# A routed expert layer around attention on one core: the first expert computed for all tokens of two batches during the first threshold search, and the last projection and the turns of batch 2 placed later

## The chip, the core and the metric

The kernel runs on one core of a Trainium2 chip. The metric is the time of one execution on the device, in microseconds (us), lower is better. The engines are TensorE (PE), VectorE (DVE), ScalarE (ACT), GpSimd (POOL) and the queue of SyncE (SP), which only starts transfers. TensorE's clock has two levels, 1.2 and 2.4 GHz; the profile gives the granted clock as a share of the higher one.

## The reference

```
B, N, D = 4, 1024, 128        # E = 8 experts, I = 512, H = 16 heads of 8
def ffn(x):                   # k = N // E * 2 = 256 tokens for each expert of each batch
    affinity = softmax(x @ gate_w.T)              # over the experts
    gating, idx = top_k(affinity.transpose(0, 2, 1), 256)
    x_in = x[b, idx]
    h = silu(x_in @ w_gate[e].T) * (x_in @ w_up[e].T)
    return zeros_like(x).at[b, idx].add(gating * (h @ w_down[e].T))
x = x + 0.5 * ffn(layernorm(x))
x = x + attention(layernorm(x))                   # 3D rotary, softmax, projection
x = x + 0.5 * ffn(layernorm(x))
```

Everything is float32 at the inputs and outputs.

## The kernel before

The work is one program of hand-placed instructions for each engine, held together by semaphores. It has three stages: expert layer, attention, expert layer.

An expert layer works on halves of the batches: half 0 is batches 0 and 1 and half 1 is batches 2 and 3. A pass `it` (0 to 15 in the first layer, 16 to 31 in the second) is one expert on one half: 512 tokens (256 of each batch). Its tokens are gathered from DRAM by four indirect transfers on POOL (`gather`), turned on PE (`turn_tokens`), put through four gate and up matmul pairs with 512 columns (`gate_up(it, u)`), Silu on ACT, the product on DVE (`hidden`), and the down matmuls (`down`), which stand in the following pass. ACT or DVE scales the result (`outputs`), and POOL adds it to DRAM by four indirect transfers (`scatter`). Each engine has five slots in a pass, `between(it, 0)` to `between(it, 4)`, into which other work is put by the table `place`.

Before any expert of a half can run, its 256 largest affinities for each expert must be found. That is the front, `("f", hh, n)`: n = 0 to 3 turn the normalised tokens, n = 4 is the softmax of the logits, n = 5 to 7 turn the affinities, n = 8 to 17 are ten search rounds (DVE counts the affinities above a candidate in `compare`, PE adds the counts over partitions, DVE makes the next candidate), and n = 18 to 20 resolve ties and rank the chosen tokens. Then DVE writes one-hot rows for each expert (`onehots`), PE compacts the token numbers with them (`compact(j)`), and DVE reads off indices and gains (`pick(j)`), for which `gather(j)` waits. `("g", hh)` are the logits.

Half 0's front runs ahead of everything in the first layer, and half 1's is placed in the slots of passes 1 to 5. In the second layer half 0's front is placed in the last part of the attention, and half 1's in passes 17 to 22. `("p", b, g)` is the output projection of half g of batch b's attention, whose input DVE or POOL makes in `context`; those of batch 3 stand in pass 16. `moments`, `deviation` (a square root on ACT, which needs another function table than Silu), `scale_and_shift` and `normalise` are the layer norm.

ACT's tables switch between Sqrt, Exp and Silu. PE, DVE and ACT execute in order, so an instruction that waits holds up all behind it. `pY` is the one PSUM bank for down products.

Of the kernel before, what the change touches and what calls it, by code (L numbers as in the profile page):

```python
# [43 lines left out]
def tables():  # L44

    place = {}
    for n in range(NF):
        place[divmod(4 + n, 4)] = ("f", 1, n)
    place[1, 4] = ("g", 1)
# [4 lines left out]
    place[16, 2], place[16, 4] = ("p", 3, 0), ("p", 3, 1)  # L54
    for n, at in enumerate([(17, 3), (17, 4), (18, 0), (18, 1), (18, 3), (18, 4)] + [(19, k) for k in range(5)] +
                           [(it, k) for it in (20, 21) for k in range(4)] + [(22, 0), (22, 1)]):
        place[at] = ("f", 3, n)
    place[18, 2] = ("g", 3)
# [35 lines left out]
def program(nc, t, x1, out, zd, qk, vp, md, ud, dd, rd):  # L94
    ctx = ExitStack()
    with ctx:
# [127 lines left out]

        pairs = {u: (scr[:, u % 2, :], scr[:, 2 + u % 2, :]) for u in range(2, 6)}
# [12 lines left out]
        hid = [Pt[:, 2 + i, :, :].rearrange("p a (b n) -> p (a b) n", b=2) for i in range(2)]  # L238

# [64 lines left out]
        s_scat = [sem(f"scat{b}") for b in range(B)]  # L304

# [42 lines left out]

        def by_batch(a):
            return a.rearrange("(b c p) d -> b p c d", c=CH, p=P)  # L350
# [35 lines left out]
        def adds_before(j):  # L386
            return 256 * (j // RUN) + 32 * (j % E)
# [7 lines left out]
        def _(sp):  # L395
# [38 lines left out]
            for h in range(2):  # L434
                sp.dma_start(x1[h], t["x"][h * HB * N:(h + 1) * HB * N, :]).then_inc(s_copy, 16)
            for a, b in ((turn[:, :], t["turn"]), (wqT[:, :, :], t["wqkT"]), (wq[:, :, :], t["wqk"]), (bq[:, :], t["bqk"]),
                         (wv[:, :], t["wv"]), (wo[:, :], t["wo"]), (bvc[:, :], t["bv"]),
                         (bo[:, :], t["bo"].partition_broadcast(P)), (cos[:, :], t["cos"]), (sin[:, :], t["sin"])):
                sp.dma_start(a, b).then_inc(s_aconst, 16)
            store_z(2)  # L440
            store_z(3)

# [104 lines left out]
            for j in range(2, 11):  # L547
                load_weights(j)
            for b in range(2):
                sp.wait_ge(s_scat[b], 256)  # L550
                load_x(b, x1_in)
# [57 lines left out]
            write_out(2)  # L609
            write_out(3)  # L610
            load_weights(18)
# [6 lines left out]
        def _(pool):  # L618
# [11 lines left out]
            def gather(j):  # L630
                p = j % 2
                if j % E == 0:
                    pool.wait_ge(s_zst, 32 * (j // E + 1))
# [9 lines left out]
            def scatter(j):  # L643
# [3 lines left out]
                if j == 0:  # L647
                    pool.wait_ge(s_copy, 32)
                for k in range(HB * SH):
                    b = batches(j)[k // SH]  # L650
                    if k % SH == 0:
                        if j >= RUN and j % E == 0:
                            pool.wait_ge(s_out[b], 16)
                        if adds_before(j):
# [33 lines left out]
            def by_slot(hh):  # L688
# [3 lines left out]
                pool.wait_ge(s_upper, hh + 1)  # L692
                GP.tensor_tensor(to[:, :, :, 1, :], v, high, ALU.mult).then_inc(s_rest_above, 1)
# [136 lines left out]
            gather(0)  # L830
            gather(1)
            by_slot(0)
            pool.wait_ge(s_aconst, 16 * 10)
            GP.tensor_tensor(bvb[:, :], ones[:, :], bvc[:, 0:1].to_broadcast([P, D]), ALU.mult).then_inc(s_bvb, 1)
            for it in range(RUN):
                if it + 2 < RUN:
                    gather(it + 2)
                if it:
# [94 lines left out]
            for b in range(B):  # L933
                pool.wait_ge(s_scat[b], 512)

        @block.scalar
        def _(act):
# [22 lines left out]
            def front(hh, n):  # L960
# [7 lines left out]
                elif n < 7:  # L968
                    act.wait_ge(*written(key))
                    S.activation(affT[:, (n - 5) * 512:(n - 4) * 512], bank_of_use(key), ACT.Copy).then_inc(s_room, 1)  # L970
# [32 lines left out]
            def between(it, k):  # L1003
# [8 lines left out]
                if (it, k) == (0, 1):  # L1012
                    deviation(2)
                    deviation(3)
                if (it, k) == (0, 3):
                    normalise(2, 0, 4)
                if (it, k) == (0, 4):
                    normalise(2, 4)
                if (it, k) == (1, 0):
                    normalise(3, 0, 4)  # L1020
                if (it, k) == (1, 1):
# [16 lines left out]
                if (it, k) == (17, 1):  # L1038
                    deviation(11)
                if (it, k) == (17, 3):  # L1040
                    normalise(11, 0, 4)
                if (it, k) == (17, 4):
                    normalise(11, 4)

            def outputs(j):
                act.wait_ge(s_down, j + 1)
                if j % RUN >= 2:
# [12 lines left out]
            def expert(it):  # L1060
                last = it + 1 in (RUN, NIT)
                for u in range(IC):
# [7 lines left out]
                    if u == 1:  # L1070
                        between(it, 1)
                        if it - 1 in SEARCH:
# [14 lines left out]
            for n in range(2, 8):  # L1087
                front(0, n)
            act.wait_ge(s_lexp, 1)
            S.activation(warm[:, :], sd[:, 0:8], ACT.Silu)  # L1090
            turn_tokens(0)
            for it in range(RUN):
# [109 lines left out]
        def _(pe):  # L1202
# [14 lines left out]
            def front(hh, n):  # L1217
# [16 lines left out]
                elif n < 7:  # L1234
                    if n == 5:
                        pe.wait_ge(s_aff, hh + 1)
                    for k in range(4):
                        last = M.transpose(bank[:, k * P:(k + 1) * P], aff[:, 4 * (n - 5) + k, :, :].rearrange("p j r -> p (j r)"),
# [810 lines left out]
```

## Time and profile before

| | us |
|---|---|
| median of three timed runs | 1197.24 (1195.34 to 1200.41) |
| the profiled execution | 1198.01 |
| its span, first to last instruction | 1196.2 |
| PE busy | 1079.0 (90%) |
| DVE busy | 909.9 (76%) |
| ACT busy | 777.1 (65%) |
| POOL busy | 614.0 (51%) |

The span is what the rows are counted in. The profiled execution has 1.8 us around its span. A busy share is a mean over three stages with different limits, so each place has to be read by itself. The mean granted clock of TensorE is 0.95 of the higher level.

### The profile page before, as it was taken

The page shows a single profiled execution, that of the slowest core. Times are in us where ns is not written, and L with a number is a line of the kernel's source. Part 1 is how long each engine was busy: PE and PEld are TensorE (multiplying, and loading weights), DVE is VectorE, ACT ScalarE, POOL GpSimd, SP SyncE. Part 2 cuts the span into 40 slices and gives each one's busy share as a digit, 9 for nine tenths or more (in the row PEclk, how much of TensorE's full clock was granted, in tenths as well). Part 3 has the DMA queues.
Part 4 walks back from the last instruction along what each step waited for, and adds up shares of the span by engine and source line. Part 5 has one row for each costly group of instructions (what it writes and reads, how often), then busy time and mean ns, then how long its engine had stood idle before and what let it go on. Part 6 is the DMA issues. An engine that isn't in the chain of part 4 may idle for free.

```text
span 1196.2 us, 23692 instructions
## 1 busy us (share of the span) xinstructions
PE 1079.0 (90%) x8860; PEld 468.3 (39%) x8860; DVE 909.9 (76%) x1491; ACT 777.1 (65%) x1471; POOL 614.0 (51%) x626
## 2 busy tenths in 40 slices
PE   6189999898699999999999999999998889999993
PEld 6066666664232222222222222222222255666752
DVE  4746755465889999999999999999997454854441
ACT  3054322542668999999989999899999835222220
POOL 4047888777689401100005446555420187677886
PEclk7589999999799999999999999999999989999997
DMA  9015456458423411121211213102210125345553
GB/s 279 30 52 126 93 112 138 91 120 220 105 85 82 94 44 28 36 63 43 54 32 22 63 43 76 27 24 63 77 45 22 28 79 121 85 92 102 113 103 30
DMA packets 93066, 93.97 MB, mean 79 GB/s; under 512 B 14684, under 2 KB 70108, under 8 KB 92920
## 3 DMA queue, kind: packets, MB, share of 16 engines
q1 hardware_dynamic: 70424, 75.67, 22.5%
q0 software_dynamic: 22528, 16.79, 10.5%
q8 instruction: 70, 1.15, 0.4%
q14 instruction: 44, 0.36, 0.1%
HBM read 64.23 MB, written 30.13 MB: 79 GB/s over the span
## 4 chain that ended last, share of the span: by engine, by line
PE 43%; DVE 18%; issue 15%; ACT 13%; POOL 6%; SPq 2%; DMA 2%; another core or an unknown queue 0%; DVEq 0%; POOLq 0%; ACTq 0%
DVE mx L1919 12%; ACT Pt L1177 11%; PE pO L1506 7%; PE pA L1366 6%; PE pS L1354 6%; PE pS L1527 4%; PE pA L1442 3%; PE pO L1355 3%; PE pS L1355 3%; POOL out_dram L662 3%; DVE ge L1602 2%; PE pA L1334 2%; POOL xg L639 2%; PE pS L1270 2%; ACT U L1168 1%
## 5 line engine op out<-in xcount | busy, mean ns | idle before, releaser
L1919 DVE TENSOR_REDUCE mx<-pA 128x2 f32<-128x1024 f32 x512 | 585.3, 1214 | 16.4 <-PE pA L1442 15.5
L1177 ACT ACTIVATE Pt<-pS 128x512 f32<-128x512 f32 x1024 | 556.3, 596 | 31.6 <-PE pS L1527 23.2
L1506 PE MATMUL pO<-Pt,Vst 128*16 128x256 f32 x4096 | 322.2, 387 | 12.5 <-ACT U L1168 12.5
L639 POOL DMA_INDIRECT xg<-zd,idx x128 | 128.2, 1001 | 145.5 <-DVE idx L1726 74.3
L1067 ACT ACTIVATE Pt<-pS 128x512 f32<-128x512 f32 x128 | 76.3, 596 | 194.6 <-PE pS L1354 160.9
L1442 PE MATMUL pA<-Kst,Qst 48*128 48x512 bf16 x704 | 137.8, 389 | 17.6 <-DVE mx L1919 14.3
L1506 PEld LDWEIGHTS pO<-Pt,Vst 128*16 128x16 f32 x4096 | 68.1, 94 | 204.9 <-issue 108.3
L1527 PE MATMUL pS<-Qst,Kst 51*128 51x512 bf16 x704 | 138.2, 389 | 5.9 <-ACT Pt L1177 2.1
L729 POOL TENSOR_TENSOR mparts<-mx,onesm 128x32 bf16<-128x32 f32 x16 | 4.0, 252 | 268.3 <-DVE mx L1924 212.0
L1354 PE MATMUL pS<-Pt,wg 128*128 128x512 f32 x256 | 138.4, 623 | 2.7 <-issue 1.4
L1366 PEld LDWEIGHTS pA<-wd,Pt 128*128 128x128 f32 x960 | 113.1, 192 | 15.6 <-issue 15.5
L662 POOL DMA_INDIRECT x<-Pt,idx x64 | 101.8, 1591 | 23.9 <-issue 20.1
L1366 PE MATMUL pA<-wd,Pt 128*128 128x128 f32 x960 | 113.9, 276 | 0.0
L1753 DVE TENSOR_TENSOR Pt<-Pt,pS 128x512 f32<-128x512 f32 x64 | 44.0, 687 | 72.1 <-PE pS L1355 44.0
L1527 PEld LDWEIGHTS pS<-Qst,Kst 51*128 51x128 bf16 x704 | 34.3, 92 | 153.2 <-ACT Pt L1177 140.3
L1753 DVE TENSOR_TENSOR Pt<-Pt,pO 128x512 f32<-128x512 f32 x64 | 43.8, 684 | 34.6 <-PE pO L1355 20.9
L1355 PE MATMUL pS<-Pt,wu 128*128 128x512 f32 x128 | 68.6, 619 | 0.0
L1355 PE MATMUL pO<-Pt,wu 128*128 128x512 f32 x128 | 65.4, 592 | 0.0
L1527 PE MATMUL pS<-pair 51*128 51x512 bf16 x320 | 62.4, 386 | 1.1 <-ACT Pt L1177 0.4
L1442 PE MATMUL pA<-pair 48*128 48x512 bf16 x320 | 61.2, 378 | 0.6 <-DVE mx L1919 0.6
L1058 ACT ACTIVATE Pt<-pA 128x512 f32<-128x512 f32 x32 | 19.1, 597 | 64.5 <-issue 40.0
L1736 DVE TENSOR_SCALAR Pt<-pA,gain 128x128 f32<-128x128 f32 x72 | 20.3, 344 | 53.1 <-PE pA L1366 37.9
(234 smaller groups left out, 1236.6 us busy)
## 6 DMA issues: line engine op xcount, KB each, us to landing
wg<-w_gate_dram SPq DMA_DIRECT2D x32, 256.0 KB
wu<-w_up_dram SPq DMA_DIRECT2D x32, 256.0 KB
wd<-w_down_dram SPq DMA_DIRECT2D x32, 256.0 KB
qk<-parts SPq DMA_DIRECT2D x64, 96.0 KB
Kst<-qk SPq DMA_DIRECT2D x132, 32.0 KB
zd<-Z SPq DMA_DIRECT2D x8, 512.0 KB
vp<-pair SPq DMA_DIRECT2D x4, 1024.0 KB, 4.3
Vst<-vp SPq DMA_DIRECT2D x16, 256.0 KB
```

Source lines behind the costliest of these rows:

```text
L639: pool.indirect_dma_start(xg[p][:, k, :], None, zd[j // E % 2], bass.IndirectOffsetOnAxis(idx[j % 6][:, k:k + 1], 0)).then_inc(s_gath[p], 16)
L662: pool.indirect_dma_start(acc, bass.IndirectOffsetOnAxis(rows[j % 6][:, k:k + 1], 0), ye[j % 2][:, k, :], None, compute_op=ALU.add).then_i ...
L1067: S.activation(sg[:, u % 2, :], pG[u % 2], ACT.Silu).then_inc(s_silu, 1)
L1177: S.activation(Pt[:, s % 4, j, r * 512:(r + 1) * 512], pS[:, bank_of(k, 4 * s + 2 * j + r), :], ACT.Exp, scale=SCALE).then_inc(s_exp, 1)
L1354: M.matmul(pG[u % 2], wg[p][:, u * P:(u + 1) * P], xt[:, p, :], start=True, stop=True).then_inc(s_gate, 1)
L1355: M.matmul(pU[u % 2], wu[p][:, u * P:(u + 1) * P], xt[:, p, :], start=True, stop=True).then_inc(s_up, 1)
L1366: last = M.matmul(pY[:, k * D:(k + 1) * D], hid[p][:, i, k * P:(k + 1) * P], wd[p][:, i, :], start=(i == 0), stop=(i == IC - 1))
L1442: last = M.matmul(pA[ring[q, a] % 2][:, r, :], Qst[k][64 * r:64 * r + 48, j, c * P:(c + 1) * P], Kst[k][64 * r:64 * r + 48, j, half * 512: ...
L1506: last = M.matmul(pO[32 * h:32 * h + 16, cols], Vst[k][:, s % 8, h, :], Pt[:, s % 4, h // 2, (h % 2) * 512 + 256 * a:(h % 2) * 512 + 256 * ...
L1527: last = M.matmul(pS[:, bank_of(k, n + r), :], Kst[k][64 * r:64 * r + ROWS, j, (s % 8) * P:(s % 8 + 1) * P], Qst[k][64 * r:64 * r + ROWS, ...
L1753: V.tensor_tensor(hid[it % 2][:, u, :], sg[:, u % 2, :], pU[u % 2], ALU.mult).then_inc(s_hid, 1)
L1919: V.reduce_max(mx2[:, k, 2 * j:2 * j + 2, c, half], pA[ring[q, a] % 2][:, :, :], AX.X).then_inc(s_Ar, 1)
```

## The change

Two things are changed.

First, expert 0 of half 0 has no pass any more. All 2048 tokens of batches 0 and 1 go through it in 16 gate and up steps (`whole_step`) and four blocks of down products (`whole_down`), which are put between the search rounds of half 0's front. ACT does its Silu (`whole_silu`) and copies the down products out of PSUM unscaled (`whole_rows`). When the search is over, DVE makes a gain for every token that is zero where the token was not chosen (`whole_gains`), and in pass 1 adds gain times row to x (`whole_sum`); SP stores the sum as the first half of the layer's result, in place of the copy of x. The first pass is now `it` = 1. Batches 2 and 3 are normalised later, and half 1's front begins one slot on.

Second, in the second layer, batch 3's projections go from slots (16, 2) and (16, 4) to (16, 4) and (17, 1), with the DVE work that belongs to them; the one-hot rows of expert 18 go into slot (16, 0); the first instructions of half 1's front go from (17, 3) to (18, 0) and on, and end at (22, 1) as before.

```diff
     place = {}
-    for n in range(NF):
-        place[divmod(4 + n, 4)] = ("f", 1, n)
-    place[1, 4] = ("g", 1)
+    for n, at in enumerate([(1, 1), (1, 2), (1, 3), (1, 4), (2, 1), (2, 2), (2, 3), (2, 4)] +
+                           [divmod(4 + n, 4) for n in range(8, NF)]):
+        place[at] = ("f", 1, n)
+    place[2, 0] = ("g", 1)
...
-    place[16, 2], place[16, 4] = ("p", 3, 0), ("p", 3, 1)
...
+    place[16, 4], place[17, 1] = ("p", 3, 0), ("p", 3, 1)
...
 # SP
-            for h in range(2):
-                sp.dma_start(x1[h], t["x"][h * HB * N:(h + 1) * HB * N, :]).then_inc(s_copy, 16)
+            sp.dma_start(x1[1], t["x"][HB * N:2 * HB * N, :]).then_inc(s_copy, 16)
...
+            for b in range(HB):
+                sp.wait_ge(s_sum, b + 1)
+                for i in range(2):
+                    sp.dma_start(x1_in[b][:, 4 * i:4 * i + 4, :], X[:, b * CH + 4 * i:b * CH + 4 * i + 4, :]).then_inc(s_init[b], 16)
...
 # ACT
+            for n in range(13, 16):
+                whole_silu(n)
+            deviation(2)
+            deviation(3)
+            whole_rows(2)
+            normalise(2, 0, 4)
+            whole_rows(3)
+            act.nop().then_inc(s_xt, 1)
+            turn_tokens(1)
+            for it in range(1, RUN):
                 expert(it)
...
-                if (it, k) == (17, 1):
+                if (it, k) == (17, 3):
                     deviation(11)
...
 # PE
+            def whole_step(n):
+                t, i = divmod(n, IC)
...
+                if n >= 2:
+                    pe.wait_ge(*step_done(s_whole_hid, s_hid, n - 2))
+                M.matmul(pG[n % 2], wg[0][:, i * P:(i + 1) * P], ZT[:, t * 512:(t + 1) * 512], start=True, stop=True
+                         ).then_inc(*step_signal(s_whole_gate, s_gate, n))
+                M.matmul(pU[n % 2], wu[0][:, i * P:(i + 1) * P], ZT[:, t * 512:(t + 1) * 512], start=True, stop=True
+                         ).then_inc(*step_signal(s_whole_up, s_up, n))
...
+            for r in range(ROUNDS):
+                front(0, 8 + r)
+                whole_step(3 + r)
+                if r >= 2:
+                    whole_down(0, 2 * (r - 2), 2 * (r - 1))
+            front(0, 8 + ROUNDS)
+            whole_down(1, 0, 6)
+            front(0, 9 + ROUNDS)
+            whole_down(1, 6, 12)
+            front(0, 10 + ROUNDS)
+            whole_down(1, 12, 16)
+            whole_step(13)
...
 # DVE
+            def whole_sum(b):
...
+                for c in range(CH):
+                    last = V.scalar_tensor_tensor(X[:, b * CH + c, :], whole_y[:, b * CH + c, :], whole_gain[:, c, b:b + 1],
+                                                  X[:, b * CH + c, :], ALU.mult, ALU.add)
...
+            for r in range(ROUNDS):
+                front(0, 8 + r)
+                whole_product(3 + r)
+            for n in range(8 + ROUNDS, NF):
+                front(0, n)
+            all_onehots(1)
+            whole_product(13)
+            pick(1)
+            all_onehots(2)
+            whole_product(14)
+            pick(2)
+            whole_product(15)
+            all_onehots(3)
+            whole_gains()
             moments(2)
             moments(3)
```

On PE, in the first search, between two rounds (the matmul from `passed` is the round's sum over partitions) there was nothing. Before:

```order
L1243 MATMUL pA<-ident,affc 32x128 x4
L1247 MATMUL pA<-passed,same_try 128x1 x10
L1250 MATMUL pA<-cgt,same_row 128x1
L1251 MATMUL pA<-ceq,earlier 128x1
L1254 MATMUL pA<-csel,earlier 128x1
L1257 MATMUL pA<-identb,slotp 128x128
```

After, two rounds of the ten and the end of the search:

```order
L1312 MATMUL pA<-passed,same_try 128x1
L1501 MATMUL pS<-ZT,wg 128x512
L1503 MATMUL pS<-ZT,wu 128x512
L1516 MATMUL pA<-wd,Pt 128x128 x2
L1315 MATMUL pA<-cgt,same_row 128x1
L1316 MATMUL pA<-ceq,earlier 128x1
L1516 MATMUL pA<-wd,Pt 128x128 x6
L1319 MATMUL pA<-csel,earlier 128x1
L1516 MATMUL pA<-wd,Pt 128x128 x6
L1322 MATMUL pA<-identb,slotp 128x128
```

A step and two down products now stand behind each round's sum, and down products behind each of the last search matmuls.

On ACT, behind the last Silu of the whole expert, with what each row waits for:

```order
L1130 ACTIVATE Pt<-pS 128x512 [waits whole_hid,gate]
L987 ACT_TABLE_LOAD
L987 ACTIVATE sd<-mv,eps 128x8 [waits ve] x2
L1134 ACTIVATE scr<-pA 128x512 [waits whole_down]
L997 ACTIVATE Z<-X,shift,rstd 128x128 [waits zst,side,shift]
L997 ACTIVATE Z<-X,shift,rstd 128x128 x3
L1134 ACTIVATE scr<-pA 128x512 [waits down]
L1096 ACTIVATE Pt<-pA 128x512 [waits xtr]
```

The two copies of down products (blocks 2 and 3, L1134) stand behind the deviations of batches 2 and 3 (L987), which wait for DVE's statistics. All of this is new at this place.

On PE, in pass 16, from the compaction of expert 18 (L1334 before, L1399 after) on. Before:

```order
L1334 MATMUL pA<-columns,room 128x10 x16
L1306 MATMUL pA<-wo,scr 128x128 x4
L1354 MATMUL pS<-Pt,wg 128x512
L1355 MATMUL pS<-Pt,wu 128x512
L1344 MATMUL pA<-ident,xg 128x128 x4
L1354 MATMUL pS<-Pt,wg 128x512
L1355 MATMUL pO<-Pt,wu 128x512
L1306 MATMUL pA<-wo,scr 128x128 x4
```

After:

```order
L1399 MATMUL pA<-columns,room 128x10 x16
L1420 MATMUL pS<-Pt,wg 128x512
L1421 MATMUL pS<-Pt,wu 128x512
L1410 MATMUL pA<-ident,xg 128x128 x4
L1420 MATMUL pS<-Pt,wg 128x512
L1421 MATMUL pO<-Pt,wu 128x512
L1371 MATMUL pA<-wo,scr 128x128 x4
L1420 MATMUL pS<-Pt,wg 128x512
L1421 MATMUL pS<-Pt,wu 128x512
L1420 MATMUL pS<-Pt,wg 128x512
L1421 MATMUL pO<-Pt,wu 128x512
L1432 MATMUL pA<-wd,Pt 128x128 x8
```

The first projection (L1306, L1371) moved behind the turn of the next expert's tokens and the last gate pair; the second now stands behind these rows, in pass 17.

## Rows read from the trace of the kernel before

**Rows 1.** Head of the page, and its granted clock in tenths, in 40 slices.

```profile
span 1196.2 us, 23692 instructions
...
PEclk7589999999799999999999999999999989999997
```

**Rows 2.** Timeline of DVE, first search: start, duration, instruction, idle before.

```profile
26.55 1.28 DVE L1602 TENSOR_SCALAR_CACHE_REDUCE ge<-ZT,digits 128x1024 bf16<-128x1024 f32 x1 [2.43 <-ACT ZT L970]
...
29.05 0.16 DVE L1639 TENSOR_SCALAR step<-pA 128x1 int32<-128x1 f32 x1 [0.38 <-PE pA L1247]
...
31.41 0.16 DVE L1639 TENSOR_SCALAR step<-pA 128x1 int32<-128x1 f32 x1 [0.36 <-PE pA L1247]
...
54.86 0.29 DVE L1664 TENSOR_SCALAR upper<-pA 128x128 bf16<-128x128 f32 x1 [0.45 <-PE pA L1257]
...
66.55 0.64 DVE L1592 BATCH_NORM_AGGREGATE mv<-stats 128x2 f32<-128x6 f32 x8
```

**Rows 3.** Timeline of PE, first search and passes 0 to 3.

```profile
23.91 1.97 PE L1238 MATMUL pA<-ident,ZT 128*128 128x128 f32 x8 [3.18 <-DVE ZT L1682]
...
60.72 3.76 PE L1414 MATMUL pA<-ones 128*128 128x128 f32 x20
...
68.68 2.07 PE L1354 MATMUL pS<-Pt,wg 128*128 128x512 f32 x2 [0.69 <-issue]
...
79.58 1.02 PE L1354 MATMUL pS<-Pt,wg 128*128 128x512 f32 x2
...
81.73 1.02 PE L1354 MATMUL pS<-Pt,wg 128*128 128x512 f32 x2
...
83.45 1.95 PE L1366 MATMUL pA<-wd,Pt 128*128 128x128 f32 x16
85.23 0.60 PE L1223 MATMUL pA<-ident,Z 128*128 128x128 f32 x4
...
109.96 0.17 PE L1247 MATMUL pA<-passed,same_try 128*128 128x1 bf16 x1
```

**Rows 4.** Windows of one us: busy time of each engine, granted clock, DMA.

```profile
63.00:64.00 1.00, 1.00 (x9) 1.00 (x9) 1.00 (x6) 0.00 (x0) 0.91 (x1) 0.79 0.21 66
...
73.00:74.00 1.00, 1.00 (x3) 0.52 (x2) 0.26 (x1) 0.00 (x0) 0.00 (x0) 0.67 0.00 0
```

**Rows 5.** Timeline of ACT, pass 0: a table load and what follows it.

```profile
74.64 1.28 ACT L944 ACT_TABLE_LOAD   x1
75.93 0.49 ACT L944 ACTIVATE sd<-mv,eps 128x8 f32<-128x8 f32 x2
```

**Rows 6.** Timeline of PE, passes 16 to 22.

```profile
970.62 1.36 PE L1306 MATMUL pA<-wo,scr 128*128 128x128 f32 x8 [3.44 <-DVE scr L1805]
...
988.02 0.60 PE L1344 MATMUL pA<-ident,xg 128*128 128x128 f32 x4
...
1008.55 0.76 PE L1238 MATMUL pA<-ident,ZT 128*128 128x128 f32 x4 [2.31 <-DVE ZT L1682]
...
1019.65 0.16 PE L1247 MATMUL pA<-passed,same_try 128*128 128x1 bf16 x1
...
1025.57 0.16 PE L1247 MATMUL pA<-passed,same_try 128*128 128x1 bf16 x1 [1.26 <-DVE passed L1607]
...
1028.21 0.16 PE L1247 MATMUL pA<-passed,same_try 128*128 128x1 bf16 x1 [0.56 <-issue]
...
1057.42 0.22 PE L1257 MATMUL pA<-identb,slotp 128*128 128x128 bf16 x1
```

**Rows 7.** Timeline of POOL, passes 16 to 31.

```profile
981.85 0.95 POOL L639 DMA_INDIRECT xg<-zd,idx  x1 [0.30 <-issue]
...
1021.20 1.01 POOL L639 DMA_INDIRECT xg<-zd,idx  x1 [5.06 <-DVE idx L1726]
...
1064.80 1.01 POOL L639 DMA_INDIRECT xg<-zd,idx  x1 [2.45 <-issue]
...
1187.83 1.55 POOL L662 DMA_INDIRECT out_dram<-Pt,idxo  x1 [0.30 <-issue]
```

More of the change, by code:

```diff
@@ L304, in program @@
         s_scat = [sem(f"scat{b}") for b in range(B)]
+        s_whole_gate = sem("whole_gate")
+        s_whole_up = sem("whole_up")
+        s_whole_silu = sem("whole_silu")
+        s_whole_hid = sem("whole_hid")
+        s_whole_down = sem("whole_down")
+        s_whole_y = sem("whole_y")
+        s_whole_gain = sem("whole_gain")
+        s_sum = sem("sum")
+        s_init = [sem(f"init{b}") for b in range(HB)]
         s_bvb = sem("bvb")
@@ L347, in program, with step_done, step_signal, block_done @@
         s_out = [sem(f"out{b}") for b in range(B)]
+        def step_done(steps, passes, n):
+            return (steps, n + 1) if n < 15 else (passes, 4)
+        def step_signal(steps, passes, n):
+            return (steps, 1) if n < 15 else (passes, 4)
+        def block_done(blocks, passes, t):
+            return (blocks, t + 1) if t < 3 else (passes, 1)
+        def block_signal(blocks, passes, t):
+            return (blocks, 1) if t < 3 else (passes, 1)
         def by_batch(a):
@@ L1046, in outputs @@
                 act.wait_ge(s_down, j + 1)
-                if j % RUN >= 2:
+                if j % RUN >= 2 and j > 2:
                     for b in batches(j - 2):
@@ L1387, in expert @@
             def expert(it):
-                first, last = it in (0, RUN), it + 1 in (RUN, NIT)
+                first, last = it in (1, RUN), it + 1 in (RUN, NIT)
                 gate_up(it, 0)
@@ new lines, in whole_down @@
+            def whole_down(t, first, end):
+                if first == 0:
+                    pe.wait_ge(*step_done(s_whole_hid, s_hid, 4 * t + 3))
+                    if t == 0:
+                        pe.wait_ge(s_wd[0], 16)
+                        pe.wait_ge(*was_read(("f", 0, 4)))
+                    else:
+                        pe.wait_ge(*block_done(s_whole_y, s_ye, t - 1))
+                for m in range(first, end):
+                    k, i = divmod(m, IC)
+                    last = M.matmul(pY[:, k * D:(k + 1) * D], whole_hid[t][i][:, k * P:(k + 1) * P], wd[0][:, i, :],
+                                    start=(i == 0), stop=(i == IC - 1))
+                if end == 16:
+                    last.then_inc(*block_signal(s_whole_down, s_down, t))
@@ L1436, in _ @@
+            front(0, 9 + ROUNDS)
[3 more added lines that the diff above has]
+            whole_step(13)
+            pe.nop().then_inc(s_comp, 1)
+            compact(1)
+            whole_step(14)
+            compact(2)
+            whole_step(15)
+            whole_down(2, 0, 16)
+            whole_down(3, 0, 16)
+            pe.nop().then_inc(s_xtr, 1)
+            turn_tokens(1)
+            for it in range(1, RUN):
                 expert(it)
```

173 lines of the change are left out of this document (106 added, 67 removed).

## The prediction

> **What bounds the kernel now.** I read the page first for span and clock [rows 1], then the timelines of DVE and PE over the first 112 us [rows 2, 3], the one-microsecond windows for the granted clock [rows 4], ScalarE's table loads [rows 5], and PE and POOL over the second expert stage [rows 6, 7]. The attention stage between them is untouched and only shifts. The chain of waits names PE for the first stage and POOL's calls for the end.
>
> The first search, 26.55 to about 54.9, is a chain of DVE and PE: a round is 31.41 - 29.05 = 2.36 us, and PE does 0.16 us in it. TensorE is at 1.2 GHz nearly all through it and up to 73 us (the 5s in the head's clock line); each time it rises some 3 to 5 us after dense work resumes (dense work from 60.72, level up in the window 63 to 64; from 68.68, up in 73 to 74) [rows 3, 4]. From pass 0 on PE is nearly never idle: the first stage is bounded by PE.
>
> The second stage is different. POOL's calls run to the end of the span, back to back (0.3 us apart) from the gather at 1064.80, and PE is done long before the last call at 1187.83 [rows 7]. What sets the end is when expert 24's gather may start, which waits for the end of the second-half search (last PE result of it 1057.42). Before that, PE stalls 3.44 us for the context product at 970.62 and 2.31 us at 1008.55 [rows 6]; POOL idles 5.06 us before 1021.20 and 2.45 before 1064.80 [rows 7]. So work saved on PE in passes 16 to 22 is worth at most POOL's idle time there.
>
> **Part 1: the search that now carries expert 0.** One step is a gate and an up matmul of 512 columns: 1.72 us at 2.4 GHz (from 81.73 to 83.45), about twice that at 1.2 (the two matmul halves of a gate took 2.07 us at 68.68, those at 81.73 took 1.02). A block's down products are 16 of 128x128, 3.57 us: half of them stand between 83.45 and 85.23 [rows 3]. So 16 steps and 4 blocks are 27.5 + 14.3 = 42 us of PE at the high level; PE had 33 us from 20.7 to 54.
> Start: steps 0 and 1 begin at 20.73 (PE was free from there: the row at 23.91 less its 3.18 of idle), ahead of the transposes that stood at 23.91. At 1.2 GHz they take 6.9 us; if the level rises after 3.5 us, they end at 20.73 + 3.5 + (3.44 - 1.75) = 25.9. The transposes then run at twice the speed, and the first scan starts at 27.8, for 26.55: 1.25 us late (bounds 0.7 and 3.7: level up after 2.5 us, or not at all).
> Rounds: each gets a product on DVE behind the scan. The second-half search has such rounds: 1025.57 to 1028.21, 2.64 us [rows 6], so + 0.28 for nine rounds, 2.5, and 0.25 for the first. PE does 1.72 + 0.45 in a round, so it fits, if the clock is high.
> After the last round PE first finishes step 12 and two down products (1.72 + 0.45 = 2.2 us), while the tie count, which needs no scan, is ready before; the product there also waits for the end of block 0, and six down products (1.34) stand ahead of each of the next two search matmuls. By these pieces I estimate + 1.35 (bounds 0.3 and 2.5). Together the search ends 5.35 us later: the first scores of slots are read at 60.2, for 54.86 [rows 2].
> From there to the first sparse pass: DVE went from 54.86 to the end of the fourth statistics, 67.19, in 12.33 us. It gets three products, the last behind a PE step that stands behind the second compaction (together about 2.6) and the gains (0.3): 15.25. ScalarE has both deviations ahead of the copy of block 2, and the copy frees the only bank that block 3 can use. So PE waits from about 11.9 to 16.3 after the slot scores, 4.4 us, and that is long enough to lose the clock (after 2.31 us without work it was lost at 1008.55: the four transposes there took 0.76 us, those at 85.23 took 0.60). Block 3 then takes 4.8 us (3.6 at the high level, 7 at the low); copy, token turn and copy 2.2. The first gate of pass 1 comes 23.35 us after the slot scores, where it came 79.58 - 54.86 = 24.7.
> Pass 1 loses pass 0's down (3.57) but has three of the four half normalisations on ScalarE, which set its length: 10.65 us. Pass 2 gets the logits matmul (1.1), and the softmax has one slot less to hide in (0.9), as has the first scan (0.4): 17.65 to the first search matmul of the second half. 23.35 + 10.65 + 17.65 = 51.65, where rows 2 and 3 give 109.96 - 54.86 = 55.1. Gain 3.45, less 5.35: the first stage is **1.9 us slower** (range 6 slower to 2 faster). It removes a whole pass of 15 us and pays it back in the search, in PE's wait and in the dense work. The two sums on DVE (16 operations, some 5 us) lie in passes 1 and 2, where it waits for PE. The copy of x that is gone from the queue freed nothing that waited; the stores that take its place are needed only at the first scatter, 25 us on. Moving x's first half is not on the path.
>
> **Part 2: passes 16 to 22.** The one-hot writes of expert 18 move into the time in which DVE waits for a transfer; the projection moves behind gates 2 and 3 (3.44 us) of pass 16, so the 3.44 us wait goes, and with it the low clock behind it. But PE then reaches expert 18's token turn at about 983.3, and the last call of its gather, held by POOL's own normalisation, is issued at 981.85; with about 2.5 us to land, the turn is at 985, for a row at 988.02 [rows 6, 7]. 3.0 us are left of more than 5.
> In pass 17 the deviation stands behind gate 2, so two table loads delay the fourth Silu, and gate 1 of pass 18 waits about 1.0 us. A table load is 1.28 us in the trace and the next activation starts 0.01 us behind it [rows 5]; with two of them and 0.3 of work the Silu is 2.9 late, 1.9 of it covered. The Trainium skill, "ScalarE: Activation LUTs", section "What ACT_TABLE_LOAD costs", adds a drain of 1.38 us to each; by that the gate would wait 3.8 us and part 2 gain 2.8 less. The trace has no such gap.
> The softmax now has gates and half a down (3.5 us) between its transposes, so the 2.31 us stall and the low clock behind it (about 1.7) go. From the turn at 985.2 PE has 30.1 us of work to the first search matmul of the half (nine gate pairs, two downs, turns, transposes, compactions), plus the 1.0: 1016.3, for 1019.65. Then the ten rounds go into fewer slots: 2.64, 3.6, 2.8, 2.7, 3.25, 2.64, 3.6, 2.8, 2.7 by the same slots of before, and 8.0 for the ties and ranks: 34.8, for 1057.42 - 1019.65 = 37.8. So the last result comes at about 1051.1, 6.3 us earlier. PE stalls more in pass 20 but runs two slots less. POOL could save its two waits, 5.06 + 2.45 = 7.5, at most; 6.3 fits below it. A short wait at the turn of 985 may cost the clock (1.5 us, one time in three). I take **6.0 us** (bounds 2 and 7.5), and the end follows one for one, since POOL's calls behind it are the same.
>
> **Sum.** 6.0 - 1.9 = 4.1 us faster. The profiled execution was 1198.01 us with a span of 1196.2, 0.8 us over the median of 1197.24. Span 1192.1, execution 1193.9; median **1193.1 us**.
>
> **Rivals.**
> - The clock stays at 1.2 GHz in the dense rounds. PE then needs 0.16 + 3.5 + 0.9 = 4.6 us for a round, 2.0 more than 2.64. Ten rounds and a late start are 20 to 23 us, so about 1213 to 1216; if only some rounds, 1200 to 1208. For it: a round leaves PE idle a fifth of its time, a third in the first two. Against it: from 1020 to 1030 PE was as idle, and gate matmuls kept 0.86 us. This decides if more than three or four rounds run low: slower. 0.15.
> - The first stage breaks even or gains (block 3 doesn't wait, or the clock isn't lost: 4.4 + 1.2 less, limited by the gathers and DVE) while part 2 gives all of POOL's idle time: 1187 to 1191. 0.30.
> - Part 2 doesn't do what it says: full rounds in 19 to 21 stall PE 1.3 us each time, as at 1025.57, and the late Silu costs all of its 2.9, where nothing covers it. Gain 2, total 1197, no change. 0.15.
> - The forecast: 0.40.
>
> **Numbers.** 0.5% is 6.0 us, about what this kernel's measurement can tell from no change: faster is below 1191.3, slower above 1203.2. The forecast's own range is 1190 to 1197. Of it some 0.05 lies below 1191.3. Faster 0.30 + 0.05 = 0.35; slower the part of the first rival beyond six microseconds, 0.12, and 0.03 for the sum of two low ends; same 0.50. Range 1187 to 1202: below it 0.06, above 0.13.
>
> **What would show it.** After: search rounds of 2.64 us between 30 and 58 us with a granted clock of 1.0 from about 24 us; slot scores near 60; PE idle over 4 us ahead of block 3; first gate of pass 1 near 83.5; first second-half search matmul near 112, for 109.96. In the second stage: no wait over 1 us at the projections, the turn of expert 18 at 985 less the shift, POOL idle ahead of expert 24's gather under 1.5 us, and from that gather to the end the same 131 us. It is wrong if rounds take over 3 us, if PE waits nowhere before pass 1, or if the second search takes more than 37 us.

## The result and the profile after

| | kernel before | kernel after |
|---|---|---|
| median of 20 runs | 1198.03 us (1195.34 to 1200.81) | 1200.49 us (1194.59 to 1204.71) |
| profiled execution | 1198.01 us, span 1196.2 | 1196.27 us, span 1194.3 |
| PE, DVE, ACT, POOL busy | 1079, 910, 777, 614 us | 1103, 920, 784, 606 us |

The ratio of after to before is 1.0022 (95% interval 1.0012 to 1.0032). With 20 runs the median of before is 1198.03 us; the prediction had 1197.24 from three. The forecast was 1193.1 us; the kernel is 2.5 us slower where 4.1 us faster was forecast. In three more timings, each beside the kernel before, the same kernel had 0.9992 (0.9976 to 1.0008), 1.0021 (1.0004 to 1.0038) and 0.9980 (0.9961 to 0.9999). Taken together this is no change by the bound of 0.5%; the forecast's 0.9966 lies in the last of the four intervals only.

The profiled execution of after is one of its short ones (among the 20, spans go from 1192.7 to 1202.8 us), and it is shorter than that of before although the median is longer. One profile cannot explain that, so later profiles of the same kernel are read beside it.

Head of the page of after:

```profile
span 1194.3 us, 23953 instructions
...
PEclk8999999999798999999999999999999989999997
```

The low slice at the start is gone [rows 1]: the first search now runs at the high level. Timeline of PE of after, first stage and second search:

```profile
23.36 1.02 PE L1501 MATMUL pS<-ZT,wg 128*128 128x512 f32 x2
...
29.03 0.17 PE L1312 MATMUL pA<-passed,same_try 128*128 128x1 bf16 x1
...
59.31 0.22 PE L1322 MATMUL pA<-identb,slotp 128*128 128x128 bf16 x1
...
63.54 1.18 PE L1399 MATMUL pA<-columns,room 128*128 128x10 bf16 x16 [1.35 <-DVE room L1828]
64.58 1.10 PE L1501 MATMUL pS<-ZT,wg 128*128 128x512 f32 x2
...
69.12 3.73 PE L1516 MATMUL pA<-wd,U 128*128 128x128 f32 x32
77.10 5.43 PE L1516 MATMUL pA<-wd,Pt 128*128 128x128 f32 x32 [4.24 <-ACT scr L1134]
...
84.05 1.12 PE L1420 MATMUL pS<-Pt,wg 128*128 128x512 f32 x2 [0.69 <-ACT Pt L1096]
...
112.16 0.18 PE L1312 MATMUL pA<-passed,same_try 128*128 128x1 bf16 x1 [0.36 <-issue]
...
985.39 0.66 PE L1410 MATMUL pA<-ident,xg 128*128 128x128 f32 x4 [1.30 <-DMA xg<-zd,idx]
...
990.43 0.63 PE L1288 MATMUL pA<-ident,Z 128*128 128x128 f32 x4 [0.95 <-POOL Z L827]
...
1001.73 0.66 PE L1288 MATMUL pA<-ident,Z 128*128 128x128 f32 x4 [1.20 <-issue]
...
1019.66 0.18 PE L1312 MATMUL pA<-passed,same_try 128*128 128x1 bf16 x1 [0.53 <-DVE affE L1751]
...
1055.62 0.22 PE L1322 MATMUL pA<-identb,slotp 128*128 128x128 bf16 x1
```

The wait ahead of block 3 (4.24 us) and its low clock are there as forecast, and the search of the second half starts at 112.16, for 109.96 [rows 3]. In the second stage no projection waits any more, but the search starts where it did (1019.66 for 1019.65), and its last result is only 1.8 us earlier (1055.62 for 1057.42) [rows 6].

Behind the slot scores, first two rows of DVE and one of POOL from before:

```profile
55.45 0.44 DVE L1670 SCALAR_TENSOR_TENSOR place_in<-upper,slotT 128x64 bf16<-128x64 bf16 x2
55.93 0.33 DVE L1700 TENSOR_TENSOR columns<-vals,upper 128x160 bf16<-128x160 bf16 x1
```

```profile
70.30 1.03 POOL L693 TENSOR_TENSOR columns<-vals,upper 128x480 bf16<-128x480 bf16 x1
```

The same place in after, DVE and then POOL:

```profile
59.57 0.29 DVE L1780 TENSOR_SCALAR upper<-pA 128x128 bf16<-128x128 f32 x1 [0.50 <-PE pA L1322]
...
60.16 1.10 DVE L1786 SCALAR_TENSOR_TENSOR place_in<-upper,slotT 128x64 bf16<-128x64 bf16 x2
61.30 1.05 DVE L1816 TENSOR_TENSOR columns<-vals,upper 128x160 bf16<-128x160 bf16 x1
```

```profile
59.94 1.02 POOL L735 TENSOR_TENSOR columns<-vals,upper 128x480 bf16<-128x480 bf16 x1 [32.73 <-DVE upper L1780]
61.04 1.13 POOL L737 TENSOR_TENSOR columns<-vals,columns 128x480 bf16<-128x480 bf16 x1
```

The change put POOL's `by_slot` (its two column products for the later experts) ahead of the gathers. It started 15.4 us behind the slot scores in before and starts 0.4 us behind them in after, so it now runs beside DVE's two groups. Each DVE group ends 0.2 to 0.3 us behind the end of a POOL operation (60.96 and 62.17), and together they take 1.4 us more, ahead of expert 1's compaction, where PE waits. I had not read this in the change.

POOL of after at the last group of experts:

```profile
1062.39 1.01 POOL L678 DMA_INDIRECT xg<-zd,idx  x1 [2.17 <-issue]
...
1185.77 1.55 POOL L703 DMA_INDIRECT out_dram<-Pt,idxo  x1 [0.30 <-issue]
```

The gather of expert 24 is 2.4 us earlier than in [rows 7] and the end follows it: 123.4 us from gather to last call, where it was 123.0. POOL still idles 2.17 us ahead of it, where under 1.5 was forecast.

### The profile page after: what moved, and what is told of

Its sections match the earlier page's. It is cut to its first block, busy times and chain, and to the rows that moved or that the text cites. A ratio compares the mean times of both kernels' runs of the same rounds, so it can differ in the third digit from the quotient of the medians.

```text
span 1194.3 us, 23953 instructions
## 1 busy us (share of the span) xinstructions
PE 1103.1 (92%) x8964; PEld 480.7 (40%) x8964; DVE 920.0 (77%) x1515; ACT 784.3 (66%) x1481; POOL 605.9 (51%) x618
## 3 DMA queue, kind: packets, MB, share of 16 engines
q0 software_dynamic: 21824, 16.27, 10.1%
## 4 chain that ended last, share of the span: by engine, by line
DVE 46%; PE 29%; issue 9%; POOL 8%; ACT 4%; DMA 1%; SPq 1%; another core or an unknown queue 0%; POOLq 0%; DVEq 0%; ACTq 0%
DVE mx L2078 37%; PE pS L1420 5%; PE pA L1432 5%; POOL out_dram L703 4%; ACT Pt L1242 3%; DVE ge L1718 3%; POOL xg L678 3%; PE pO L1421 2%; PE pS L1421 2%; PE pO L1622 2%; PE pS L1335 2%; PE pA L1558 2%; PE pS L1643 1%; PE pA L1399 1%; PE pA L1516 1%
## 5 line engine op out<-in xcount | busy, mean ns | idle before, releaser
L1105 ACT ACTIVATE Pt<-pS 128x512 f32<-128x512 f32 x124 | 73.9, 597 | 187.0 <-PE pS L1420 169.3
L678 POOL DMA_INDIRECT xg<-zd,idx x124 | 124.0, 1000 | 121.2 <-DVE idx L1842 70.8
L1558 PE MATMUL pA<-Kst,Qst 48*128 48x512 bf16 x704 | 137.7, 389 | 17.5 <-DVE mx L2078 14.1
L1420 PE MATMUL pS<-Pt,wg 128*128 128x512 f32 x248 | 131.7, 613 | 2.3 <-DVE Pt L1869 1.3
L1432 PEld LDWEIGHTS pA<-wd,Pt 128*128 128x128 f32 x928 | 109.4, 192 | 14.9 <-issue 14.8
L1432 PE MATMUL pA<-wd,Pt 128*128 128x128 f32 x928 | 110.2, 275 | 0.0
L703 POOL DMA_INDIRECT x<-Pt,idx x60 | 95.4, 1590 | 23.0 <-issue 17.9
L1643 PEld LDWEIGHTS pS<-Qst,Kst 51*128 51x128 bf16 x704 | 34.3, 92 | 152.3 <-ACT Pt L1242 140.2
L1869 DVE TENSOR_TENSOR Pt<-Pt,pO 128x512 f32<-128x512 f32 x62 | 42.5, 686 | 34.7 <-PE pO L1421 19.6
L1421 PE MATMUL pS<-Pt,wu 128*128 128x512 f32 x124 | 64.0, 598 | 0.0
L703 POOL DMA_INDIRECT out_dram<-Pt,idx x32 | 51.9, 1621 | 9.8 <-issue 9.4
```

Source lines behind the costliest of these rows:

```text
L678: pool.indirect_dma_start(xg[p][:, k, :], None, zd[j // E % 2], bass.IndirectOffsetOnAxis(idx[j % 6][:, k:k + 1], 0)).then_inc(s_gath[p], 16)
L703: pool.indirect_dma_start(acc, bass.IndirectOffsetOnAxis(rows[j % 6][:, k:k + 1], 0), ye[j % 2][:, k, :], None, compute_op=ALU.add).then_i ...
L1105: S.activation(sg[:, u % 2, :], pG[u % 2], ACT.Silu).then_inc(s_silu, 1)
L1420: M.matmul(pG[u % 2], wg[p][:, u * P:(u + 1) * P], xt[:, p, :], start=True, stop=True).then_inc(s_gate, 1)
L1421: M.matmul(pU[u % 2], wu[p][:, u * P:(u + 1) * P], xt[:, p, :], start=True, stop=True).then_inc(s_up, 1)
L1432: last = M.matmul(pY[:, k * D:(k + 1) * D], hid[p][:, i, k * P:(k + 1) * P], wd[p][:, i, :], start=(i == 0), stop=(i == IC - 1))
```

## The experiments

All ratios are to the kernel before, timed on the same chip; runs e1 to e4, e5 to e8, e9 to e12 and e13 to e16 shared a chip each. "Part 1" is the first expert layer's share of the change, "part 2" the second's.

**The parts alone (e1, e2).** Each keeps one half of the diff.

```
 e1: place[16, 2], place[16, 4] = ("p", 3, 0), ("p", 3, 1)      # second stage as before, with all that belongs to it
 e2: for it in range(RUN): expert(it)                           # first stage as before
```

> Part 1 of the change alone; the second expert stage as before. Theory A (timetable): the first stage is 1.4 us longer up to the start of attention, as in the profile of after, and that is all, so ratio about 1.001 (+1.4 us), and spans spread no wider than before's. Theory B (clock): the dense first stage of the change loses the high level of the clock in part of its executions, which the profiled one did not show; then part 1 alone is 4 to 6 us slower in the median (ratio 1.0035 to 1.005), its spans spread over some 10 us and the longer ones have the lower mean clock.

> Part 2 alone, first stage as before. Theory A: the profile of after shows the second stage 2.5 us shorter (start of pass 16 at +0.64, end at -1.9), so -2.5 us, ratio 0.998. Theory B says the same of this part, with before's narrow spread. A third theory, that the spread and the loss come from part 2 (late turns and late search in passes 18 to 22), gives 0 to +2 us here and nothing lost in part 1.

Part 1 alone has 1.0035 (1.0015 to 1.0054), 4.2 us slower; part 2 alone 0.9963 (0.9949 to 0.9977), 4.4 us faster. Again on another chip:

> Part 2 alone, the kernel of e2 (0.9963). 3 to 5 us below the kernel before. If the mended part 1 is worth what the start of attention says (285 to 287 us for 289 to 291), e14 is 2 to 3 us below this one; if the second stage hides it, the two are equal.

It had 0.9957 (0.9940 to 0.9975). So both signs were forecast rightly, and both sizes came out on the unfavourable side: part 1 cost 4.2 us, not 1.9, and part 2 gave 4.4 to 5.2, not 6.0. The intervals are wide: 1.8 to 6.5 us for part 1, 2.8 to 6.1 and 3.0 to 7.2 for part 2, so each forecast size alone lies just inside. The two medians together make 0.2 us or 1 us faster, which fits "no change" and not 4.1 us faster. Whether part 1 also widens the spread can't be told: e1's 12 runs cover 9.9 us and e2's 5.5, but the kernel before, with 27 to 35 runs in each of the four sets, covers 8.0 to 10.1 us.

**Other executions of the kernel after (e4, e12, e16).** The same kernel, to see what differs from run to run.

> The kernel after unchanged, for another profiled execution. Theory B: if this execution is longer than 1197 us, its granted clock is below 1.0 in some windows between 24 and 90 us, or from 955 us on, where the first profile had 1.0, and the start of attention is later than 288.4 by the difference. Theory A: the windows are the same as in the first profile, and the difference lies in the attention stage.

> The kernel after, unchanged. By the sum of the parts run alone (4.2 us lost, 4.4 us gained) it is within 1.5 us of the kernel before; by the first timing it is 2.6 us slower. If the execution is again of 1197 us or more, the first search starts near 30.3 and the steps behind expert 1's compaction run at the low clock; if it is near 1194, it starts near 29 and they run at the high one.

> The kernel after, unchanged, on the chip of the other three: 0 to 2.6 us above the kernel before, 4 to 6 us above e15.

They had spans of 1197.4, 1197.9 and 1198.8 us. Timeline of PE of e4:

```profile
24.29 1.40 PE L1501 MATMUL pS<-ZT,wg 128*128 128x512 f32 x2
...
30.33 0.17 PE L1312 MATMUL pA<-passed,same_try 128*128 128x1 bf16 x1
...
64.82 1.18 PE L1399 MATMUL pA<-columns,room 128*128 128x10 bf16 x16 [1.34 <-DVE room L1828]
65.86 1.94 PE L1501 MATMUL pS<-ZT,wg 128*128 128x512 f32 x2
67.59 1.92 PE L1503 MATMUL pS<-ZT,wu 128*128 128x512 f32 x2
...
80.04 5.25 PE L1516 MATMUL pA<-wd,Pt 128*128 128x128 f32 x32 [4.24 <-ACT scr L1134]
...
86.81 1.13 PE L1420 MATMUL pS<-Pt,wg 128*128 128x512 f32 x2 [0.69 <-ACT Pt L1096]
```

Windows of e4 and then of after (busy time of PE, PE loads, DVE, ACT and POOL, granted clock, DMA):

```profile
24.00:25.00 1.00, 1.00 (x2) 0.34 (x1) 0.68 (x4) 0.00 (x0) 0.48 (x2) 0.50 0.71 230
...
66.00:69.00 3.00, 3.00 (x5) 1.07 (x5) 1.60 (x5) 0.60 (x1) 1.33 (x1) 0.50 0.00 0
```

```profile
24.00:25.00 1.00, 1.00 (x3) 0.33 (x2) 0.32 (x1) 0.58 (x1) 0.86 (x3) 1.00 0.61 199
...
30.00:60.00 30.00, 26.20 (x114) 15.10 (x113) 26.52 (x90) 6.57 (x11) 0.06 (x1) 1.00 0.01 3
...
66.00:69.00 3.00, 3.00 (x22) 1.88 (x21) 1.50 (x5) 0.80 (x2) 2.30 (x2) 1.00 0.08 22
```

Two things differ. The clock rises about two microseconds later (at 25.0 for 23.0), so the first scan result comes at 30.33, for 29.03. And behind the gap of 1.34 us at expert 1's compaction the clock is at its lower level from 66 to 69, where it stayed high in the first profile: the pair of gate matmuls takes 1.94 us for 1.10, and the first gate of pass 1 comes another 1.5 us later. e1 and e12 have the same rows within 0.3 us; in e16 the low stretch begins at 67.3 and ends in block 2. So the first profile of after showed a lucky execution. The second-half search starts at 112.16 there, and at 114.84 to 116.22 in the other four.

**ScalarE's order (e3).** The forecast put PE's wait ahead of block 3 on this order.

```
-            deviation(2)
-            deviation(3)
             whole_rows(2)
+            deviation(2)
+            deviation(3)
-            normalise(2, 0, 4)
             whole_rows(3)
+            normalise(2, 0, 4)
```

> The kernel after with ScalarE's copy of down block 2 ahead of the two deviations, and that of block 3 ahead of the first normalisation. If the 4.24 us wait of PE and the low clock of block 3 (5.43 us for 3.6) lie on the path, the first gate of pass 1 comes 4 to 6 us earlier than 84.05; then the end of the first stage gains 3 to 5 us if nothing else is late, 0 to 1 if the gathers of passes 2 and 3 or the normalisations take its place. Against the kernel before: 1197 to 1200 for theory gained-back-later, 1194 to 1196 if it is kept.

0.9963 (0.9951 to 0.9975): 4.0 us below the kernel after on the same chip, kept to the end. PE of e3:

```profile
65.21 1.17 PE L1399 MATMUL pA<-columns,room 128*128 128x10 bf16 x16 [1.33 <-DVE room L1828]
...
67.26 1.91 PE L1503 MATMUL pS<-ZT,wu 128*128 128x512 f32 x2
...
78.21 3.81 PE L1516 MATMUL pA<-wd,Pt 128*128 128x128 f32 x32 [0.78 <-ACT scr L1134]
```

The wait ahead of block 3 is 0.78 us for 4.24, and block 3 takes 3.81 us. The gap of 1.33 us at the compaction is still there, and behind it the clock is low from 67.1 to 73.9.

**Filling the gap at the compaction (e5).** Step 14 goes ahead of `compact(1)`, with e3's order.

> The kernel with the down rows copied first, and gate and up step 14 put ahead of expert 1's compaction, where PE idles 1.3 to 1.4 us for the one-hot rows. Theory clock-after-gap: in three of four profiled executions with the first part of the change, the steps behind that compaction run at the low level (1.9 us for a matmul pair that takes 1.0), 1.7 to 3.5 us in all; with the gap filled they run at 1.0 us and the first gate of pass 1 comes 2 to 3 us earlier, ratio to the kernel before about 0.994 to 0.995 (the version without this edit had 0.9963). Rival: DVE's one-hot rows and picks set the pace there, PE's time behind the gap is hidden, and the ratio stays at 0.996.

0.9973 (0.9953 to 0.9993), no better than e3. PE of e5:

```profile
67.61 1.18 PE L1399 MATMUL pA<-columns,room 128*128 128x10 bf16 x16 [1.23 <-DVE room L1828]
...
70.95 4.87 PE L1516 MATMUL pA<-wd,U 128*128 128x128 f32 x32
...
83.11 1.66 PE L1420 MATMUL pS<-Pt,wg 128*128 128x512 f32 x2 [1.38 <-ACT Pt L1096]
```

The gap did not go, it moved: 1.23 us now stand ahead of expert 2's compaction, and the clock is low behind that instead (the 32 down matmuls of block 2 took 4.87 us for 3.73). The first gate of pass 1 still came 22.0 us behind the slot scores, for 23.5 in e3, but the clock fell a second time there, behind a wait of 1.38 us, and the search of the second half was no earlier than in e3 (112.90 for 112.81). In the other profiles with this order the same wait of 1.38 us kept the clock. This run does not speak against the price of the low clock; it failed to remove it.

**POOL's products held back (e6, e13, e14, e10).** `by_slot(0)` on POOL waits for DVE's own column products; e6 and e14 have e3's order too, e13 has the order of after.

```
                 pool.wait_ge(s_vals, 6 * hh + 6)
+                if hh == 0:
+                    pool.wait_ge(s_two, 1)
```

> The kernel with the down rows copied first, and POOL's column products of experts 2 to 7 begun only when DVE has written its own. In after, the two run at once and DVE's place_in and columns take 1.10 and 1.05 us, for 0.44 and 0.33 before. Theory contention: they take 0.44 and 0.33 again, expert 1's compaction and gather come 1.3 us earlier and the first stage gains 0.5 to 1.3 us. Rival: the slowness only moves to the one-hot rows, which then run beside POOL, and nothing is gained.

> The kernel after with POOL's column products held until DVE has written its own, and nothing else changed. Theory: the contention cost 1.4 us on DVE ahead of expert 1's compaction, and the longer gap costs the clock behind it (1.7 us in most executions): 2 to 3 us less than the kernel after, while the 4.24 us wait ahead of block 3 stays. Rival: ScalarE's order sets the end of this stretch whatever happens ahead of it, and nothing is gained.

> Hold and copies first, the kernel of e6, which had 0.9949. If that ratio is real, 5 to 6 us below the kernel before here too; by the like kernel e10 it is 3 us below. Against e13 the order is worth 3 to 4 us.

DVE of e6:

```profile
60.22 0.45 DVE L1788 SCALAR_TENSOR_TENSOR place_in<-upper,slotT 128x64 bf16<-128x64 bf16 x2
60.70 0.34 DVE L1818 TENSOR_TENSOR columns<-vals,upper 128x160 bf16<-128x160 bf16 x1
...
61.39 2.12 DVE L1830 TENSOR_TENSOR room<-slots,place_in 128x1024 bf16<-128x1024 bf16 x2
```

PE of e6 and then of e13:

```profile
63.56 0.67 PE L1401 MATMUL pA<-columns,room 128*128 128x10 bf16 x8 [0.71 <-DVE room L1830]
64.09 1.10 PE L1503 MATMUL pS<-ZT,wg 128*128 128x512 f32 x2
...
73.16 3.81 PE L1518 MATMUL pA<-wd,Pt 128*128 128x128 f32 x32 [0.78 <-ACT scr L1136]
...
79.66 1.12 PE L1422 MATMUL pS<-Pt,wg 128*128 128x512 f32 x2 [1.38 <-ACT Pt L1098]
```

```profile
76.88 6.43 PE L1518 MATMUL pA<-wd,Pt 128*128 128x128 f32 x32 [4.24 <-ACT scr L1136]
```

The two DVE groups are back at 0.45 and 0.34 us; part of the contention moves to the one-hot rows (2.12 us for 1.29). What counts more is that the compaction starts with its first half while the rows of the second are written, so the longest gap there is 0.71 us, and the pair of gate matmuls behind it takes 1.10 us. Both profiles, e6 and e14, show that, as does e13. On one chip: after 1197.08, e13 1197.12, e14 1191.34 (0.9924, 0.9898 to 0.9950, six runs), e15 1194.53. So the hold alone gave nothing that the timing shows: the wait of 4.24 us stayed, and the clock fell 1.3 us ahead of block 3 and stayed low for nearly all of it, 6.43 us for 5.43 in after. Order and hold together gave 5.7 us. e6 had 0.9949 (0.9931 to 0.9968).

Holding POOL longer, until expert 1's one-hot rows are written:

> Both parts, copies first, and POOL's column products held until expert 1's one-hot rows are written, where the version before held them only until DVE's columns. There the one-hot rows took 2.12 us, for 1.29 without POOL beside them. Theory contention: they take 1.29 us again, expert 1's compaction ends 0.8 us earlier, PE's gap there shrinks; 0 to 1 us better than 0.9949, so 0.994 to 0.995. Rival: expert 2's compaction now waits for POOL's columns, and the ratio is 0.995 to 0.996.

0.9975 (0.9959 to 0.9990). Expert 1's rows took 1.29 us, expert 2's 2.12: the contention moved once more. The attention starts at 286.69, like in e14 (286.55), so why this ratio is weaker than those of e6 and e14 stays open; they were timed in three sets of runs, and e10's profile takes 4 to 5 us more in the attention than theirs, as all of its set do (see below).

**Part 1 with both mends, alone (e9).** With the longer hold.

> Part 1 alone, with ScalarE's copies of the down rows first and POOL's column products held until expert 1's one-hot rows are written; second stage as before. Part 1 as given cost 4.2 us alone (1.0035). If its price is the wait ahead of block 3, the low clock behind both gaps and the contention (4.2 + 1.5 + 1.7 + 1.4, of which some is hidden), the mended part 1 is 1 to 3 us faster than before: ratio 0.998 to 0.999. Rival: the search's own price (5.35 us later by the extra products and the low-clock start) outweighs the saved pass anyway: ratio 1.000 to 1.002.

0.9993 (0.9975 to 1.0010), between the two theories. Beside e1 the mends are worth 5 us of ratio, but the two were timed in different sets of runs.

**POOL's chain in the second stage (e7, e8).** Part 2 alone, with expert 18's gather inside POOL's normalisation; e8 also takes one Newton step for the inverse square root instead of four, which leaves the normalised rows of that batch slightly off.

```
                 link(GP.tensor_scalar(xmean[:, :], xsum[:, :], 1.0 / D, None, ALU.mult))
+                if between is not None:
+                    gather(between)
...
-                for n in range(4):
+                for n in range(1 if i == 10 else 4):                    # e8 only
```

> Part 2 alone, with expert 18's gather put in the middle of POOL's own normalisation, as soon as its indices are there. Theory POOL-chain: with part 2 the front of the second half is bound by POOL's normalised rows of batch 2 (its first transposes wait for them at 990.4 in after), not by PE or by the gather. Then the token turn of expert 18 comes at about 981 to 982 without a wait, the first transposes of the front wait 2 to 3 us for POOL's rows instead, and the search starts where it did: ratio 0.996 as for part 2 alone, at best 1 us better where a clock loss at the turn is avoided. Rival (my forecast's view, PE work from the turn on): all comes 2 to 3 us earlier, ratio 0.994.

> As the last one, and POOL's inverse square root for batch 2 takes one Newton step instead of four, so the normalised rows of that batch are slightly off (left out: 12 small operations of 0.28 us). Theory POOL-chain: POOL's rows come 3.4 us earlier, the first transposes of the front with them by 2 to 3 us (to about 986.5 less the shift), and the end of the search and the last gathers follow by 1.5 to 3 us against the run beside it. If PE were the bound, the two runs would have the same end.

They have 0.9959 (0.9944 to 0.9974) and 0.9947 (0.9929 to 0.9965), medians 1193.24 and 1191.65. PE of e7 and then of e8:

```profile
984.82 0.60 PE L1346 MATMUL pA<-ident,xg 128*128 128x128 f32 x4
...
990.50 0.63 PE L1225 MATMUL pA<-ident,Z 128*128 128x128 f32 x4 [1.23 <-POOL Z L787]
```

```profile
984.84 0.60 PE L1346 MATMUL pA<-ident,xg 128*128 128x128 f32 x4
...
989.13 0.60 PE L1225 MATMUL pA<-ident,Z 128*128 128x128 f32 x4
```

In e7 the turn no longer waits, and the front's first transposes wait for POOL's rows instead; the time is that of part 2 alone. In e8 that wait is gone too and the search starts at 1017.63, for 1018.76; the median is 1.6 us shorter, though the two intervals overlap. So POOL's normalisation holds the front by about a microsecond once the turn is early. PE's own work is next: of e8's 32.8 us from the turn to the search PE waits 1.35.

**Both, with e7's gather (e11).**

> As e10, and expert 18's gather in the middle of POOL's normalisation. Alone that edit gave 0.4 to 1 us at most in the second stage, since POOL's normalised rows still hold the front; here the same, so 0.9935 to 0.995 against the kernel before, 10 us below the kernel after only if the parts add up.

0.9983 (0.9966 to 1.0000): nothing added to e10. The version with the best measured time is that of e6 and e14.

## Why the prediction was wrong

Two terms failed, both told below: the stretch from the slot scores to pass 1 (with a smaller miss in the search), and the stretch from the turn of expert 18 to the second search, where no wait was counted.

**The search.** Right in kind. The rounds take 2.63 us with the clock at 1.00 from 30 to 60, so the rival of a low clock in dense rounds fell in every profile. Its price was 6.05 us for 5.35: from the first scan result to the slot scores' matmul 30.28 us for 25.79 in all profiles (4.5, I had 4.1), and the first scan result at 30.3 in the median of 13 profiles with part 1, for 28.8 in five without it (1.55, I had 1.25; 0.3 in the best case).

**From the slot scores to pass 1: the step that failed.** I had 23.35 us from slot scores to first gate, a gain of 1.35. The profile of after has 24.5 us, e4 has 25.95. The wait itself (4.4 forecast, 4.24) and block 3 (4.8 forecast, 5.2 to 5.4) were sized nearly rightly. Missing were the contention on DVE (1.4 us), which I had at nothing without looking at what POOL does beside it, and the low clock behind the gap at the compaction (1.5 us in four of five profiles), where I counted PE's work at the high level. In after the wait ends 17.5 us behind the slot scores, where I had 16.3; block 3 takes 0.6 us more than forecast and the copies and the turn 0.7 less. Passes 1 and 2 were right: 28.1 us to the second half's search, where I had 28.3. So the first stage is 5.0 us behind there in the median of five profiles (114.87 for 109.84), not 1.9.

**A gain I did not see.** Of those 5.0 us some 2.8 come back before attention by the medians (292.87 for 290.65). Four of the five profiles without part 1 (e2, e7, e8, e15) have PE wait 2.0 to 2.9 us for the gather of expert 11, at 207 to 209 us, as in e7:

```profile
208.68 0.65 PE L1346 MATMUL pA<-ident,xg 128*128 128x128 f32 x4 [2.87 <-DMA xg<-zd,idx]
```

None of the 13 with part 1 has this wait. Part 1 takes eight calls (four gathers and four scatters) out of POOL's queue, which is how I read this; no run tests it. The profile of before, on which my sum was built, is the one without part 1 that lacks the wait, and it started attention 3.6 us earlier than the median of its kind.

These medians mix two kinds of execution, and the kind goes by the set of runs, not by the kernel. From the start of attention to pass 16's first gate, before, after and e9 to e12 take 674.1 to 675.6 us, and the twelve others 670.5 to 672.4; e12 and e4 are the same kernel on the same chip, with 675.0 and 672.4. The same six share a wait of DVE of 2.6 to 2.7 us ahead of scaling a down product, at 202 to 209 us, where the eight others with part 1 wait 0.9 to 1.1. What differs between the sets stays open, and before is the only kernel without part 1 profiled in the longer kind, so its missing wait may belong to the kind. So single profiles of different sets must not be subtracted: e1 and e2, of one set, start attention at 292.87 and 288.64, 4.2 us apart. That is close to what the timing gives for part 1, but it is one pair.

**Part 2.** Four of its claims held: the waits at the projections and at the softmax are gone, the turn came at 985.39 (forecast 985, held by the gather), the late Silu cost nothing in after and 1.19 us ahead of a gate in e10 (forecast 1.0), and the search took 34.7 to 36.0 us (forecast 34.8, before 37.8). The failed step is "30.1 us of work to the first search matmul". With the late Silu that was 31.1; it took 34.3 (985.39 to 1019.66). PE waited 0.95 us for POOL's rows, 1.20 ahead of another transpose and 0.53 ahead of the search matmul itself, and I had counted no wait. Without these 2.7 us it is 31.6, so the work was sized rightly and the waits were missing; e7 and e8 bear out the first for about a microsecond, the other two no run tests. (A smaller slip: the "more than 5" us at the turn are 4.7 by the prediction's own rows, 988.02 - 983.3. The sum did not use it.) So the search starts no earlier in after's profile, and what shows is the denser slots: from pass 16's first gate to POOL's last call 223.0 us in the median of the 12 profiles with part 2 as it stands (221.2 to 225.5), and 225.3, 225.3 and 222.8 in the three without it. The timing gives part 2 4.4 to 5.2 us. Where the other 2 to 3 lie I could not find.

**The range and the rivals.** The median lies in the range, though the time moved the other way; that is the width of the range and no merit of the forecast. The outcome is no rival of mine: it is the forecast's mechanisms with part 1 dearer and part 2 smaller. The closest was "part 2 doesn't deliver", with 1197.

The table loads: at 84.02 in after one takes 1.28 us and the Silu follows at 85.31. By the Trainium skill, "ScalarE: Activation LUTs", section "What ACT_TABLE_LOAD costs", there would be a drain of 1.38 us more; the trace of after, like that of before, has no such gap, and the measurement decides.

## What to carry to other kernels

Price what an edit moves on an engine that runs beside the critical one, too: two POOL operations started 15 us earlier, and two groups of DVE's operations at the one place where PE waited for them took nearly three times as long. Look at more than one profile before you call a gap harmless: behind the same gap of 1.34 us the clock was low in most executions here and not in the first one profiled. Where one stretch has several waits, try the mends together as well as alone: here one alone was worth 4 us and the other nothing that shows, and both 5.7, though the 4 and the 5.7 come from different chips. When PE's waits in front of a point are removed, ask which other engine delivers what PE uses there.

## What the runs showed of the hardware

DVE operations with two inputs and POOL's products held each other up here, one whole operation at a time: 0.44 and 0.33 us became 1.10 and 1.05 (of the first group's two operations one took 0.93 us and the other 0.26). In e6 a POOL product of 1.02 took 1.42, while two one-hot writes that take 1.29 together took 2.12. The Trainium skill, "SBUF — State Buffer", section "Who interferes with whom", says that a DVE instruction with two SBUF inputs contends with a GpSimd instruction that reads SBUF, and calls the port pair that they share an exclusive lock; the trace agrees, since each DVE group ends 0.2 to 0.3 us behind the end of a POOL operation.

TensorE's granted clock stayed at 1.00 from 30 to 60 us in after, through the search rounds, where PE is busy 26.2 of 30 us. Behind the gap of 1.33 to 1.35 us at expert 1's compaction it fell to the lower level in five of six profiles (e1, e3, e4, e12, e16; not the first of after). Where the edits made that gap shorter it was kept at that place in all six profiles: at 0.7 us in e6, e13 and e14, and at no more than 0.26 us in e9, e10 and e11.
